# Passes on zeros ahead of the first data, and two copies moved ahead of a split, in a kernel of split projections and pair scores

## The reference

```python
Kf = jnp.einsum('bjd,ed->bje', F, K_w)
S = jnp.einsum('bid,bjd->bij', F, Kf)
out = jnp.einsum('bij,ijd->bid', S, W)
out = out + jnp.einsum('bid,ed->bie', F, Q_w)
```

## Time and profile before

| | us |
|---|---|
| median of 3 runs | 658.76 |
| lowest, highest | 658.09, 658.76 |
| the profiled execution's own time | 658.4 |
| its span, first to last instruction | 656.6 |
| time around the span | 1.8 |
| mean granted TensorE clock | 0.987 |

### The profile page before, as it was taken

How to read it: one execution, slowest core, us unless ns; L and a number is a source line. 1 busy time by engine, 2 the same in 40 slices (tenths; PEclk the granted TensorE clock), 3 DMA queues, 4 the chain that set the end, 5 groups by cost and what they waited for, 6 DMA issues and landing times. The chain is left out here.

```text
span 656.6 us, 18892 instructions
## 1 busy us (share of the span) xinstructions
PE 629.2 (96%) x7680; PEld 534.5 (81%) x7680; DVE 454.0 (69%) x644; ACT 429.4 (65%) x645; POOL 0.2 (0%) x4
## 2 busy tenths in 40 slices
PE   6999969999999999999999999999999999799985
PEld 4788858888888888888888888888888888688874
DVE  1767746776776776677677677677767767476755
ACT  5986647766766766766776676676676667366620
POOL 0000000000000000000000000000000000000000
PEclk9999989999999999999999999999999999799998
DMA  8946647667666766866766676676676677367337
GB/s 280 219 152 193 214 124 244 201 220 222 216 211 212 245 195 205 248 198 210 231 215 206 218 228 200 211 246 201 206 241 200 212 227 218 133 198 225 129 125 262
DMA packets 48910, 136.90 MB, mean 208 GB/s; under 512 B 3184, under 2 KB 7536, under 8 KB 40816
## 3 DMA queue, kind: packets, MB, share of 16 engines
q1 hardware_dynamic: 48880, 136.46, 65.9%
HBM read 69.34 MB, written 67.11 MB: 208 GB/s over the span
## 5 line engine op out<-in xcount | busy, mean ns | idle before, releaser
L184 ACT ACTIVATE kf<-kq_ps 128x512 f32<-128x512 f32 x256 | 153.0, 598 | 173.4 <-PE kq_ps L298 157.8
L262 DVE TENSOR_TENSOR o_sb<-o_ps,q_out 128x1024 f32<-128x1024 f32 x128 | 151.0, 1220 | 55.9 <-issue 30.9
L192 ACT ACTIVATE q_out<-kq_ps 128x512 f32<-128x512 f32 x256 | 153.0, 598 | 21.7 <-PE kq_ps L298 0.6
L237 DVE TENSOR_TENSOR f_lo<-f_ring,f_hi 128x1024 fp32r<-128x1024 f32 x126 | 147.8, 1213 | 5.7 <-ACT f_hi L177 5.7
L360 PE MATMUL o_ps<-s_t,w_sb 64*128 64x128 f32 x2048 | 135.1, 283 | 3.5 <-DVE s_t L253 2.8
L360 PEld LDWEIGHTS o_ps<-s_t,w_sb 64*128 64x128 f32 x2048 | 122.7, 192 | 8.5 <-DVE s_t L253 3.0
L177 ACT ACTIVATE f_hi<-f_ring 128x1024 fp32r<-128x1024 f32 x126 | 125.7, 1049 | 2.2 <-issue 2.2
L296 PE MATMUL kq_ps<-f_hi,k_hi 128*128 128x512 f32 x256 | 107.5, 420 | 7.0 <-DVE f_lo L229 6.1
L251 DVE COPY s_t<-o_ps 128x256 f32<-128x256 f32 x64 | 27.1, 424 | 125.9 <-PE o_ps L339 125.9
L296 PE MATMUL kq_ps<-f_hi,q_hi 128*128 128x512 f32 x256 | 101.0, 394 | 0.3 <-ACT kf L184 0.3
L298 PE MATMUL kq_ps<-f_hi,k_lo 128*128 128x512 f32 x256 | 100.9, 394 | 0.0
(11 more groups left out here) (18 smaller groups left out, 239.6 us busy)
## 6 DMA issues: line engine op xcount, KB each, us to landing
out<-o_sb SPq DMA_DIRECT2D x128, 512.0 KB, 3.9
f_ring<-f_t SPq DMA_DIRECT2D x63, 1024.0 KB, 6.5
w_sb<-w SPq DMA_DIRECT2D x2, 1024.0 KB, 17.8
f_ring<-f_t SPq DMA_DIRECT2D x4, 256.0 KB, 4.2
k_raw<-k_t SPq DMA_DIRECT2D x1, 64.0 KB, 3.2
q_raw<-q_t SPq DMA_DIRECT2D x1, 64.0 KB, 3.8
```

Source lines behind the costliest of these rows:

```text
L184: nc.scalar.activation(kf[:, c // 2, c % 2 * CK:(c % 2 + 1) * CK, :, :].rearrange("d k h i -> d (k h i)"), kq_ps[:, bank, :], COPY).then_i ...
L192: nc.scalar.activation(q_out[:, parity, :, :].rearrange("d i (h b) -> d i h b", h=2)[:, :, :, at:at + CK], kq_ps[:, bank, :].rearrange("d ...
L237: nc.vector.tensor_tensor(f_lo[:, p % 2 * 2 + e, :], f_ring[:, p % RING, e, :, :, :].rearrange("d k h i -> d (k h i)"), f_hi[:, p % 2 * 2 ...
L262: nc.vector.tensor_tensor(o_sb[:, slot, :, :], o_banks(e)[:, :, :], q_out[:, parity, :, :].rearrange("d (s m) b -> d s (m b)", s=2)[:, :, ...
```

## The change

A tile `zeros` of 128 x 512 elements is added, with a semaphore. VectorE fills it with zeros as its first instruction. TensorE waits for that and runs eleven matmuls of 512 columns on it, in fp32r, into bank `s2_ps`, whose content nobody reads; then it goes on as before. On ScalarE, the copies of products 1 and 2 are made between the splits of chunks 2 and 3, and the other six copies follow the split of chunk 3.

```diff
--- before.py
+++ after.py
@@ -26,6 +26,7 @@
 CK = BANK // (2 * N)
 RING = 4
 OBUF = 4
+WARM = 11
 
 STEP = 2 * UNITS
 
@@ -60,6 +61,8 @@
         q_hi = sbuf("q_hi", [D, D], F32R)
         q_lo = sbuf("q_lo", [D, D], F32R)
 
+        zeros = sbuf("zeros", [D, BANK], F32R)
+
 
 
         kq_ps = psum("kq_ps", [D, 3, BANK])
@@ -74,6 +77,7 @@
 
         khi_done, klo_done = sem("khi_done"), sem("klo_done")
         qhi_done, qlo_done = sem("qhi_done"), sem("qlo_done")
+        zeros_done = sem("zeros_done")
         fhi_first, flo_first = sem("fhi_first"), sem("flo_first")
         fhi_done, flo_done = sem("fhi_done"), sem("flo_done")
         k_done, kf_copied = sem("k_done"), sem("kf_copied")
@@ -193,8 +197,8 @@
                     q_out[:, parity, :, :].rearrange("d i (h b) -> d i h b", h=2)[:, :, :, at:at + CK],
                     kq_ps[:, bank, :].rearrange("d (k h i) -> d i h k", k=CK, h=2), COPY).then_inc(q_copied, 1)
 
-            def copy_pair(t, p, parity):
-                for c in range(CHUNKS):
+            def copy_pair(t, p, parity, begin=0, end=CHUNKS):
+                for c in range(begin, end):
                     copy_kf(t, p, c, 2 * c % 3)
                     copy_q(t, p, c, (2 * c + 1) % 3, parity)
 
@@ -205,8 +209,9 @@
             act.wait_ge(q_in, 16)
             nc.scalar.activation(q_hi[:, :], q_raw[:, :], COPY).then_inc(qhi_done, 1)
             split_first(2)
+            copy_pair(0, 0, 0, 0, 1)
             split_first(3)
-            copy_pair(0, 0, 0)
+            copy_pair(0, 0, 0, 1, CHUNKS)
             split_f(0, 1)
 
             def body(t, parity):
@@ -264,6 +269,7 @@
                     q_out[:, parity, :, :].rearrange("d (s m) b -> d s (m b)", s=2)[:, :, u * IR * P:(u + 1) * IR * P],
                     ALU.add).then_inc(out_done, 2)
 
+            nc.vector.memset(zeros[:, :].bitcast(F32), 0.0).then_inc(zeros_done, 1)
             dve.wait_ge(khi_done, 1)
             nc.vector.tensor_tensor(k_lo[:, :], k_raw[:, :], k_hi[:, :].bitcast(F32),
                                     ALU.subtract).then_inc(klo_done, 1)
@@ -372,6 +378,10 @@
                     if front(t, p + 1):
                         project(t, p + 1)
 
+
+            pe.wait_ge(zeros_done, 1)
+            for n in range(WARM):
+                nc.tensor.matmul(s2_ps[:, 0, :], zeros[:, :P], zeros[:, :], start=True, stop=True)
             pe.wait_ge(klo_done, 1)
             project(0, 0)
             body(0, 0)
```

## The result

The kernel after takes 649.43 us (median of four; 648.42 to 650.26), and the kernel before, measured beside it, 658.42. The ratio is 0.9869, with a 95% interval of 0.9845 to 0.9892. The forecast was 656.9 and its range went down to 656.1. The gain is 9.0 us by the medians, 8.6 by the ratio, instead of 1.85. The profiled execution took 649.57 and its span is 647.8, 8.8 us shorter than before.

A forecast was written before the change was run, and what follows sets the result against it. TensorE, busy 96% of the 656.6 us span, was taken as the bound. Memset 0, passes 0, start -1.85 and 0 later sum to -1.85 us, giving 656.9; the range ran from 656.1 to 658.6.

The forecast's parts named there:

- The passes bring the clock: TensorE's start: eleven passes on zeros from about 1.5 us raise the clock at about 7.05, ahead of product 2; price 0.
- Zeros don't bring the clock: Rival at TensorE's start: low clock lasts to 11.6, only ScalarE's order helps; gain 0.35, 658.4 us; chance 0.11.
- The memset: VectorE's first instruction: zeros ready at about 1.45 us, taking 0.69 us; cost on the path 0.
- The order on ScalarE: First pair: product 4 starts at 8.9 instead of 10.59; with the faster clock, the last pass starts 1.85 us earlier.
- It carries: Behind the first pair: no later load becomes a wait, so the 1.85 us won at the start is kept.
- The stall of 5.1 us ahead of 90.38 and the slow stretch behind it stay, only earlier: TensorE at the loop's entry: stall unchanged, near 83.4, with the slow stretch behind it; change 0.
- 0 later: Last term of the sum: nothing gained or lost behind the start, 0 us.
- That stall goes: Rival at the loop's entry: the code shift brings the loop's head in time; 650.2 us; chance 0.02.
- one more code fetch: Rival: 22 more instructions ahead of the loop add another stall, 5.1 plus up to 1.6 us; 663.6 us; chance 0.06.

The follow-up runs named there:

- front_10: The kernel before with 10 more instructions, waits on the high part of K, at the very head of TensorE's code: 660.11 us.
- tiny_passes: The kernel after with each of the eleven passes on zeros cut from 512 to 8 columns, TensorE's code otherwise the same: 651.17 us.
- passes_only: The kernel before with only the eleven passes on zeros, the old order on ScalarE: 650.84 us, ratio 0.9876.
- front_13: The kernel before with 13 more instructions, met waits, at the head of TensorE's code: 657.63 us.
- front_18: The kernel before with 18 more instructions, met waits, at the head of TensorE's code: 652.12 us.
- code_plus22: The kernel before with 22 more TensorE instructions, waits met long ago, spread over the projections of the first two tiles: 660.43 us, ratio 1.0018.
- after_plus234: The kernel after with 234 more TensorE instructions, waits met long ago, 256 more than the kernel before: 657.51 us.
- after_unrolled: The kernel after with TensorE's loop written out straight, the other engines keeping theirs: 642.81 us, ratio to before 0.9763.

## Why the prediction was wrong

- **The passes bring the clock: right, but not by the time it used.** They began at 1.46 for 1.5. The text carried 5.55 us over from before, from the first pass to the rise, and got 7.05. The fast spacing is there at 6.20, so the rise came at most 4.7 us after the first pass on zeros. Nor is 5.55 a fixed time: front_10 has its first pass at 5.91 and the rise near 15.4, with a longer pause in between (0.95 us for 0.29). The difference cost nothing here, because product 2 waits until 7.42 for another reason. The first real pass was late by 0.15, as said, and covered. "Zeros don't bring the clock" (0.11) fell: with the same code but passes of 8 columns, tiny_passes has the long spacing at 6.40, and after has the short one.
- **The memset: price 0.48 instead of 0.69,** free as said.
- **The order on ScalarE: right.** Product 4 at 8.91 for 8.9, last start at 12.49 for 12.51. The passes with the old order were never priced, and passes_only shows that they can lose their clock again.
- **It carries: right.** No load became a wait. The text gave the margins of the first and the third load (1.6 and 2.2 us) and left out the tightest, the second: it was issued at 4.01, took 10.4 to land, and its split begins in after at 15.3, so the margin is 0.9.
- **"The stall of 5.1 us ahead of 90.38 and the slow stretch behind it stay, only earlier": wrong,** and nearly the whole error. In the sum it is the "0 later". The stall went with its slow stretch: 5.1 + 1.5 = 6.6 us. The text had the mechanism as a rival, "That stall goes", with 650.2, which is 0.8 from what was measured, and gave it 0.02. The failed step is the one ahead of that number. It saw that 22 instructions were added ahead of a branch at which TensorE already stood for a fetch, and that they could shift the code either way, but it had no row for how near to free the present stall was, and put the term at nothing all the same. Its reason was the fixed slot of the loop's head. The slot is the same in front_13 and front_18, and five instructions ahead of the loop decide between a stall of 5.0 us and none: what counts is how much code stands ahead of the branch, and this is what the change moved. Why code_plus22 stalls with as many instructions as the kernel after stays open.
- **The rival "one more code fetch" (663.6)** had the same mechanism with the other sign. In the runs no kernel has a second stall of 5 us at the entry. after_plus234 only brings back the first, 657.51 for 649.43, and the nearest to a stall in straight code is the 1.34 us of code_plus22.

## What to carry to other kernels

Where an engine stands still at a loop's entry for nothing that the profile shows, with a packet of an instruction queue in the gap, an edit of the code ahead of the loop may remove that stall or bring it back. The edit will then be credited or blamed for time that isn't its own, 6.6 us here. Compare such kernels with padded code or with the loop written out before saying what an edit is worth. Writing the loop of the busiest engine out took both stalls away here: 658 to 644.5 with no other change.

## What the runs showed that I had not expected

- Five instructions more (13 to 18) ahead of a loop were worth 5.5 us, one execution each, and 6.5 us at the loop's entry itself. They stand where TensorE waits for data in any case.
- The stall behind the loop's exit, 4.5 to 4.8 us, is in every kernel with the loop, with a packet of q8 in it (at 559 in before, 551 in after). With its slow stretch it costs about 7 us (after against after_unrolled: 649.43 to 642.81).
- TensorE's clock fell again in the profiled run of passes_only, about 1 us after TensorE had restarted from 1.99 us of idleness. After 5 us of waiting at the loop's entry it was at 0.71 of full speed over the 5.42 us that followed.
